# Reordering the front work of a Mamba scan step: earlier slots, an earlier Silu, and four decays kept in SBUF

## What is computed

```python
xc, z = split(x @ in_proj_w.T)
xc = silu(causal_conv4(xc, conv_w) + conv_b)
dt, Bm, Cm = split(xc @ x_proj_w.T)          # 16, 16, 16 columns
dt = softplus(dt @ dt_proj_w.T + dt_proj_b)
dA = exp(dt * A)                             # the decays, one for each channel and state
h_t = dA_t * h_(t-1) + dt_t * Bm_t * xc_t    # a scan over the tokens
y = sum over states of (h * Cm) + xc * Dp
out = (y * silu(z)) @ out_proj_w.T
```

## Time and profile before

| what | value |
|---|---|
| median of 3 runs | 8325.03 us (8324.12 to 8332.88) |
| the profiled execution's own time | 8328.63 us |
| its span, first to last instruction | 8326.8 us |
| busy in the span | PE 7047.6, DVE 6032.8, ACT 4649.6, POOL 5789.0 us |
| mean granted clock of PE | 0.906 of full |

### The profile page before, as it was taken

The page is one execution under the profiler, slowest core; times in us unless marked ns, Lnnn a source line. Parts: engine busy times, 40 slices in busy tenths (PEclk is TensorE's granted clock), DMA queues, the critical chain, the costliest instruction groups (busy, mean ns, idle before and its releaser), DMA issues. The chain is left out here.

```text
span 8326.8 us, 150231 instructions
## 1 busy us (share of the span) xinstructions
PE 7047.6 (85%) x47940; PEld 4977.0 (60%) x47940; DVE 6032.8 (72%) x8278; ACT 4649.6 (56%) x7795; POOL 5789.0 (70%) x4008
## 2 busy tenths in 40 slices
PE   8799999999999984788878888888888885766993
PEld 6677777777777762455555555555555554545882
DVE  4477777767777764899989899989999897640116
ACT  2376767667677653666666666666656663211223
POOL 0177777777777762999889898898989896322005
PEclk9899999999999986888888898888988897988996
DMA  3301011010010014111122111221112211332213
GB/s 103 101 0 26 0 26 26 0 26 12 13 26 0 6 56 157 69 65 61 60 68 71 65 55 66 68 72 64 54 66 68 72 62 53 139 129 95 68 56 125
DMA packets 175723, 489.44 MB, mean 59 GB/s; under 512 B 31894, under 2 KB 70452, under 8 KB 154160
## 3 DMA queue, kind: packets, MB, share of 16 engines
q1 hardware_dynamic: 158256, 442.45, 16.4%
q10 hardware_dynamic: 10880, 25.28, 0.8%
q0 software_dynamic: 6144, 16.33, 0.6%
HBM read 360.72 MB, written 123.73 MB: 58 GB/s over the span
## 5 line engine op out<-in xcount | busy, mean ns | idle before, releaser
L1439 POOL TENSOR_TENSOR hh<-dtx,bb 128x1024 f32<-128x1024 f32 x1024 | 2403.9, 2368 | 337.5 <-PE mb_ps_y L1147 332.6
L1516 DVE TENSOR_TENSOR_SCAN hh<-mb_ps_da,state,hh 128x512 f32<-128x512 f32 x2048 | 2490.8, 1266 | 162.1 <-ACT mb_ps_da L1308 96.2
L638 POOL TENSOR_TENSOR p_lo<-p_turned 128x512 bf16<-128x512 f32 x2048 | 2064.8, 1039 | 590.8 <-ACT p_turned L602 573.8
L1308 ACT ACTIVATE mb_ps_da<-dt,amat 128x512 f32<-128x512 f32 x2048 | 1393.9, 686 | 1168.0 <-DVE hh L1516 1160.2
L656 DVE TENSOR_SCALAR_CACHE_REDUCE prob<-ps_s 128x1024 f32<-128x1024 f32 x1024 | 1213.2, 1222 | 395.7 <-PE ps_s L537 395.7
L1147 PEld LDWEIGHTS mb_ps_y<-ident,hh 128*128 128x128 f32 x8192 | 1043.8, 153 | 617.3 <-issue 376.8
L1147 PE MATMUL mb_ps_y<-ident,hh 128*128 128x128 f32 x8192 | 1180.2, 294 | 185.6 <-ACT dt L1322 110.1
L545 PE MATMUL ps_t<-ident,prob 128*128 128x128 f32 x8192 | 1310.1, 283 | 3.5 <-issue 2.7
L602 ACT ACTIVATE p_turned<-ps_t 128x512 f32<-128x512 f32 x1280 | 762.7, 596 | 810.9 <-PE ps_t L545 810.9
L596 ACT ACTIVATE prob<-prob,nmx 128x1024 f32<-128x1024 f32 x1024 | 1165.8, 1141 | 30.7 <-DVE nmx L661 29.4
L545 PEld LDWEIGHTS ps_t<-ident,prob 128*128 128x128 f32 x8192 | 861.6, 141 | 390.9 <-issue 377.7
(11 more groups left out here) (226 smaller groups left out, 8259.4 us busy)
## 6 DMA issues: line engine op xcount, KB each, us to landing
bb<-mb_bc SPq DMA_DIRECT2D x128, 1024.0 KB, 4.7
cc<-mb_bc SPq DMA_DIRECT2D x256, 256.0 KB, 3.1
q_head<-q_full SPq DMA_DIRECT2D x16, 1024.0 KB, 17.0
mb_u<-u SPq DMA_DIRECT2D x32, 512.0 KB, 3.3
m_dirs<-dtx SPq DMA_DIRECT2D x32, 512.0 KB, 8.3
ex_w<-in_L_ffn_w SPq DMA_DIRECT2D x16, 1024.0 KB, 7.5
xbuf<-ml_zero SPq DMA_DIRECT2D x16, 640.0 KB, 5.5
ex_xr<-xbuf SPq DMA_DIRECT2D x40, 256.0 KB, 2.7
```

Of the source, the lines that this page charges most:

```text
L638: pool.tensor_tensor(lo[:, k % RING, :], pt[:, k % RING, :], hi_view[:, k % RING, 1::2], ALU.subtract).then_inc(lo_ready, 1)
L1308: act.activation(ps_da[:, exp_bank(e), :], dt[:, j, blk, :], ACT.Exp, scale=amat[:, j, blk, r % S:r % S + 1]).then_inc(da_ready, 1)
L1439: pool.tensor_tensor(hh[:, r % RING], dtx[:, j, half(r // S)], bb[:, r % S, :].unsqueeze(1).broadcast_to([P, HK, CH]), ALU.mult).then_inc( ...
L1516: dve.tensor_tensor_scan(h, a, h, state[:, s.j, q % S, blk:blk + 1], ALU.mult, ALU.add).then_inc(scanned, 1)
```

## The change

The order tuples get other slots. The convolutions, x_proj, dt_proj and the copies stand up to four slots sooner, Silu at slot 14 instead of 16. POOL's `residual` moves from slot 22 to 20 and ACT's `xp_part2` from slot 23 to 19. The in_proj of the next x stands one slot sooner. The decays of slots 16 and 17 (`EARLY`) are made at slot 14, ahead of Silu, into the free `xpre` in SBUF, without a wait on a scan; the scans of these two slots read them there. The other 60 decays of a step take the three PSUM banks in turn. No instruction is added or removed.

```diff
-    PE_CONV, PE_Z, PE_OUT, PE_XP = ((0, 1), (3, 4), (8, 9), (12, 13)), (10, 11, 13, 14), ((15, 16), (17, 18)), (19, 20)
-    PE_DT, PE_X = (21, 21, 22, 22), (27, 28, 29, 30)
-    ACT_CONV, ACT_Z, ACT_OUT, ACT_XP = (5, 5, 10, 14), (11, 12, 14, 15), (17, 19), 21
-    ACT_DT, ACT_X = (22, 22, 23, 23), (28, 29, 30, 31)
-    SILU_AT, PART2_AT, SOFT_AT = 16, 23, (23, 24)
-    TAKE_AT, PE_BACK, GATE_AT, FREE_AT = (20, 4), ((23, 24), (6, 7)), ((25, 26), (7, 8)), ((26, 27), (8, 9))
-    RES_AT, SPLIT_AT, DTADD_AT, DTX_AT = 22, 24, (25, 0), (27, 2)
+    PE_CONV, PE_Z, PE_OUT, PE_XP = ((0, 1), (2, 3), (7, 8), (9, 10)), (8, 10, 11, 12), ((13, 14), (17, 18)), (15, 16)
+    PE_DT, PE_X = (19, 19, 20, 20), (26, 27, 28, 29)
+    ACT_CONV, ACT_Z, ACT_OUT, ACT_XP = (2, 4, 9, 11), (10, 11, 12, 13), (15, 18), 17
+    ACT_DT, ACT_X = (20, 20, 21, 21), (27, 28, 29, 30)
+    SILU_AT, PART2_AT, SOFT_AT = 14, 19, (22, 23)
+    TAKE_AT, PE_BACK, GATE_AT, FREE_AT = (20, 4), ((22, 23), (5, 6)), ((24, 25), (6, 7)), ((25, 26), (7, 8))
+    RES_AT, SPLIT_AT, DTADD_AT, DTX_AT = 20, 22, (25, 0), (27, 2)
+
+    EARLY = (SILU_AT + 2, SILU_AT + 3)
...
-    def exp_bank(e):
-        return 1 if e == 2 * SLOTS - 1 else e % 3
+    IN_PSUM = [e for e in range(2 * SLOTS) if e // HK not in EARLY]
 
     def exp_after(e):
-        earlier = [p for p in range(e) if exp_bank(p) == exp_bank(e)]
-        return earlier[-1] if earlier else [p for p in range(2 * SLOTS) if exp_bank(p) == exp_bank(e)][-1] - 2 * SLOTS
+
+        i = IN_PSUM.index(e)
+        return IN_PSUM[i - 3] if i >= 3 else IN_PSUM[i - 3] - 2 * SLOTS
+
+    def decay(e):
+
+        if e // HK in EARLY:
+            return xpre[:, e - HK * EARLY[0], 0:CH]
+        return ps_da[:, IN_PSUM.index(e) % 3, :]
...
-                    act.wait_ge(scanned, ONE + k * SLOTS * 2 + exp_after(e) + 1 + 4)
+                    if r not in EARLY:
+                        act.wait_ge(scanned, ONE + k * SLOTS * 2 + exp_after(e) + 1 + 4)
                     blk = HK * (r // S) + kk
-                    act.activation(ps_da[:, exp_bank(e), :], dt[:, j, blk, :], ACT.Exp,
+                    act.activation(decay(e), dt[:, j, blk, :], ACT.Exp,
...
-                    if q + 1 < SLOTS or s.front:
+                    if (q + 1 < SLOTS or s.front) and q + 1 not in EARLY:
                         decays(s, q + 1)
+                    if q == SILU_AT:
+                        for r in EARLY:
+                            decays(s, r)
...
-                    h, a = hh[:, q % RING, kk, :], ps_da[:, exp_bank(e), :]
+                    h, a = hh[:, q % RING, kk, :], decay(e)
```

## The result

The changed kernel takes **8770.12 us** (median of 4 runs, 8766.63 to 8770.75) against 8324.58 for the kernel before beside it: a ratio of 1.0533 [1.0515, 1.0551], or 445 us more. The forecast was 8675 in a range of 8430 to 8830. The direction and most of the places were right; the size was short by 95 us, 3 us a step.

The account below looks back on a forecast made before the run. DVE, with least to spare, was taken as the bound. Its waits summed to 21.2 us a step against 9.9, +11.3 in 31 steps or +350 us: 8675 us beside the median of 8325, range 8430 to 8830.

Parts of the forecast that it names:

- Slot 20: DVE's output of slot 18 waits for ACT's save, behind `xp_part2` waiting for POOL's residual: 3.4 us a step.
- slot 21: The C of slot 19 comes late behind dt_proj's blocks, with PE at half clock: 7.0 us a step.
- full-clock rival: PE stays at full clock through the new gaps: +6.5 us a step, 8525 us; chance 0.10.
- Slot 17: Scans of slot 17, both tensors in SBUF, contend with POOL: 3.0 us a step.
- Silu and slot 16: Silu's wait stays and moves to DVE's output of slot 14, behind the scans of slot 16: 4.5 us.
- the slower of the two cases named: Half of x_proj, a sum and the C behind Silu run at half clock, twice the full-clock times.
- The start of a step: PE starts after the bank of `back` is freed, as before; slots 8 to 12 cost 3.0 us a step.
- Slots 8 to 12: PE has 7.1 us of work between two Cs, DVE 5.8, twice: 3.0 us of waits a step.
- The loop's end: The last x copy and halo come a slot sooner: 0.3 of 1.1 us a step is left.
- The 9.9: DVE's waits a step in the kernel before that an order can move: C, decays and save, 9.9 us.
- No contention: Rival: scans from SBUF don't contend with POOL, 3.0 us a step less, 8580 us; chance 0.14.
- The faster case: Rival: the residual is done before ACT reaches slot 19, -1.6 us a step, 8275 us; chance 0.09.

Follow-up runs that it names:

- e1: The changed kernel with `xp_part2` on ACT at slot 21 instead of 19, nothing else: 8564.08 us, ratio 1.029.
- e3: The kernel before with the early decays alone (slots 18 and 19, made ahead of Silu at 16 into SBUF): 8590.72 us, ratio 1.0321.
- e5: The kernel before with the change's early slots 0 to 13 alone (convolutions, z pieces, copies, back work of the last step): 8460.18 us, ratio 1.0166.
- e4: The kernel before with only the last x piece, its copy and the halo a slot sooner: 8311.31 us, ratio 0.998.
- e8: The kernel before with the last x pieces sooner, and C of slot 21 instead of slot 15 multiplied on POOL: 8293.22 us, ratio 0.9965.
- e10: The changed kernel with all decays in PSUM, `xp_part2` and dt_proj's second half later, start of the step at old slots or one sooner: 8319.16 us, ratio 0.9985.

## Why the prediction was right, and where it was too small

- **The bound.** DVE's lost time is the measure, as argued from the earlier trace rows: 13.5 us more a step gives 432 of the 445 us.
- **Slot 20 (forecast 3.4) and slot 21 (7.0)** were right: 3.3 and 7.5, with ACT's wait for POOL's `xf` and PE's restart at half clock as described. The full-clock rival fell: the dt blocks took 3.78 us after 10.81 idle, as the ones of the earlier trace rows. The two hang together, as the working had it when it counted the C "behind the save": e1 takes 3.1 off the first and 1.8 off the second with one edit. Not seen, here or in e1's expectation, were the 1.3 that this edit also takes off at slots 5 and 8.
- **Slot 17 (3.0)** was right in size: 2.9. By the rule of the Trainium skill (SBUF — State Buffer, "Who interferes with whom") it would have been 3.5, by the prediction's estimate. POOL's instruction beside a scan (here of slot 16) grew from 2.36 to 3.28:

```profile
5047.03 2.37 POOL L1457 TENSOR_TENSOR hh<-hh,cc 128x1024 f32<-128x1024 f32 x1
5049.35 3.28 POOL L1451 TENSOR_TENSOR hh<-dtx,bb 128x1024 f32<-128x1024 f32 x1
```

  That is 0.92 for a scan of 1.2, most of it and not all. The Trainium skill is right there that two SBUF inputs contend with POOL's reads: in e3 a pair took 2.45 us with POOL idle and 15.14 beside POOL's work.
- **Silu and slot 16 (4.5)** was right in size and in cause: 4.35. ACT's save ended at 5053.03, 3.3 us after the scans would have ended at their usual length (forecast 3.5). PE idled 3.36 us for Silu (forecast 3.3), and the C behind half of x_proj at 3.46, the slower of the two cases named, came last. The scans of slot 16 took 4.0 us more than usual and ended 0.35 us before the output began, so they "lie in the wait just named and cost nothing on DVE", by a narrow margin. In e3 the pair stood 15.14 us, and such a pair would not have fitted; that it did here is luck, as the working had no length for this pair.
- **The start of a step** is the term that was mis-sized, and it holds nearly all that is missing. Slots 8 to 12 were put at 3.0 and are 3.8; slots 5 and 6, where the back work and its gates moved a slot sooner, had no term and cost 1.0 to 2.0. The working had "PE starts after the bank of `back` is freed, as before"; but with the move the output at slot 5 waits for its C, and the gate behind it for `back`. e5 shows the group alone: 4.8 us a step at slots 5 to 12, where the sum had 3.0.
- **The loop's end (0.3)** is 0.4; e4 confirms this piece alone.
- **The rivals.** No contention fell with the scans of 3.1 us on average. The faster case fell because POOL was late at the residual; e1 takes POOL out of it and is still 236 us slower than before, so that condition would not have been enough.
- **Sum.** Forecast 21.2 lost a step, measured 24.0 on average and 24.2 in the step shown. The 3.0 between forecast and that step are 2.0 from slots 5 and 6, 0.8 from slots 8 to 12 and 0.5 from slot 21, less 0.3 from the other terms. The 9.9 set against it were counted a little low, as said above: with 10.5 the measured loss is 13.5 a step, against the 11.3 forecast.

## What to carry to other kernels

Before a piece is moved sooner, price what it needs at the new place on every queue it passes: here the one copy that came to wait for POOL cost 206 us of the 445, through everything that stood behind it in ACT's order. A wait that is as long as the work on the engine in front of it (Silu and its table loads) moves with that work; here it shrank where the waiting engine was given something to do ahead of it (e8) or came to it later (e10). And a buffer moved from PSUM to SBUF to save a wait can cost more than the wait, if its reader then shares SBUF with another busy engine, as the scans of e3 do with POOL.

## What the runs showed of the hardware

I had not expected that a DVE scan with both inputs in SBUF can be passed over again and again. In e3 a pair of scans stood 15.14 us while POOL ran five further instructions of 2.4 us without a pause; in 30 of the changed kernel's 32 steps the two pairs took 6.4 and 5.4 us, and in the first and the last step the first pair took 18.75 and 14.46. Where the scan got its turn, POOL's instruction beside it was drawn out by 0.92. With POOL idle a pair took 2.45. With the decay in PSUM the same instruction takes 1.2 us beside the same POOL work. What decides which engine goes next was not tried and stays open.
